# A transformer block with conditioned scales and shifts: the first two modulation vectors made as rows and turned upright

## The reference

```python
mod = silu(c) @ ada_w.T + ada_b                 # c: (2, 576), ada_w: (6*576, 576)
shift_msa, scale_msa, gate_msa, shift_mlp, scale_mlp, gate_mlp = split(mod, 6)
h = rmsnorm(x, g1) * (1 + scale_msa) + shift_msa
q, k, v = split(h @ qkv_w.T + qkv_b)            # q and k are normed per head, times qg and kg
x = x + tanh(gate_msa) * (softmax(q k^T / 6) v @ proj_w.T + proj_b)
h2 = rmsnorm(x, g2) * (1 + scale_mlp) + shift_mlp
x = x + tanh(gate_mlp) * (gelu(h2 @ fc1_w.T + fc1_b) @ fc2_w.T + fc2_b)
```

## Time and profile before

| | |
|---|---|
| median of 3 runs | 2911.23 us (2911.23 to 2912.59) |
| the profiled execution, its own time | 2911.72 us |
| its span, first to last instruction | 2909.9 us |
| busy in the span | PE 99%, PE weight loads 75%, DVE 68%, ACT 54%, POOL 7% |
| mean granted TensorE clock over the span | 0.992 of full speed |
| chain that ended last, by engine | PE 94%, DVE 3%, ACT 1%, DMA 1% |

### The profile page before, as it was taken

The page is one execution under the profiler, slowest core; times in us unless marked ns, Lnnn a source line. Parts: engine busy times, 40 slices in busy tenths (PEclk is TensorE's granted clock), DMA queues, the critical chain, the costliest instruction groups (busy, mean ns, idle before and its releaser), DMA issues.

```text
span 2909.9 us, 35292 instructions
## 1 busy us (share of the span) xinstructions
PE 2878.8 (99%) x12990; PEld 2174.7 (75%) x12990; DVE 1972.3 (68%) x2726; ACT 1578.1 (54%) x1922; POOL 209.9 (7%) x155
## 2 busy tenths in 40 slices
PE   8999999999999999999999999999999999999999
PEld 7999986666666666666666666788888888888887
DVE  7777778899888888888888887844344343434342
ACT  4334326776677677677677666634344343434342
POOL 1323310101000000000000000090000000000000
PEclk8999999999999999999999999999999999999999
DMA  6555554322322222222222223432222222322121
GB/s 229 163 191 172 174 168 132 88 73 63 84 78 77 78 83 63 77 84 78 73 78 69 76 82 91 133 128 86 74 86 74 82 78 90 99 85 86 41 68 50
DMA packets 238454, 282.67 MB, mean 97 GB/s; under 512 B 34960, under 2 KB 144016, under 8 KB 237392
## 3 DMA queue, kind: packets, MB, share of 16 engines
q1 hardware_dynamic: 233696, 271.33, 30.0%
q10 hardware_dynamic: 4592, 9.18, 0.9%
HBM read 195.50 MB, written 84.67 MB: 96 GB/s over the span
## 4 chain that ended last, share of the span: by engine, by line
PE 94%; DVE 3%; ACT 1%; DMA 1%; issue 0%; SPq 0%; DVEq 0%; ACTq 0%
PE ps L1539 16%; PE ps L1564 16%; PE ps L1627 15%; PE ps L1609 15%; PE ps L1551 13%; PE ps L721 12%; PE ps L1585 4%; PE ps L1550 2%; PE ps L685 1%; ACT gated L1230 1%; DMA gain<-kg 0%; DVE p_lo L1356 0%; DVE x L1416 0%; PE ps L677 0%; DVE w_lo L1409 0%
## 5 line engine op out<-in xcount | busy, mean ns | idle before, releaser
L1174 ACT ACTIVATE p_r<-ps 128x1024 f32<-128x1024 f32 x512 | 491.9, 1025 | 406.4 <-PE ps L1539 406.4
L1356 DVE TENSOR_TENSOR p_lo<-p_r,p_hi 128x1024 fp32r<-128x1024 f32 x512 | 613.4, 1219 | 0.0
L1539 PE MATMUL ps<-qT,kT 110*128 110x512 f32 x2048 | 574.9, 398 | 1.4 <-DVE aw L614 0.9
L1174 ACT ACTIVATE prob<-ps 128x1024 f32<-128x1024 f32 x512 | 483.6, 1031 | 2.3 <-PE ps L1539 2.0
L1539 PEld LDWEIGHTS ps<-qT,kT 110*128 110x128 f32 x2048 | 382.9, 190 | 136.3 <-issue 51.4
L1550 PE MATMUL ps<-prob,vp 128*64 128x512 f32 x1024 | 453.1, 595 | 0.0
L1551 PE MATMUL ps<-prob,vp 128*37 128x512 f32 x1024 | 451.7, 594 | 0.0
L1486 DVE TENSOR_TENSOR a_lo<-act,a_hi 128x512 fp32r<-128x512 f32 x144 | 101.2, 702 | 506.0 <-ACT a_hi L1217 506.0
L1350 DVE CAST p_hi<-p_r 128x1024 fp32r<-128x1024 f32 x512 | 350.2, 694 | 134.9 <-ACT p_r L1174 133.5
L1627 PE MATMUL ps<-a_hi,w 128*128 128x512 f32 x1296 | 415.5, 393 | 0.0
L1564 PE MATMUL ps<-p_hi,vx 128*128 128x512 f32 x1024 | 404.6, 395 | 0.1
(11 more groups left out here) (177 smaller groups left out, 3552.7 us busy)
## 6 DMA issues: line engine op xcount, KB each, us to landing
w_raw<-w SPq DMA_DIRECT2D x144, 320.0 KB, 2.8
qk_hi_scratch<-aw SPq DMA_DIRECT2D x32, 576.0 KB, 3.2
qk_lo_scratch<-aw SPq DMA_DIRECT2D x32, 576.0 KB, 4.4
kT<-qk_hi_scratch SPq DMA_DIRECT2D x128, 144.0 KB
qT<-qk_hi_scratch SPq DMA_DIRECT2D x128, 144.0 KB
v_scratch<-stv SPq DMA_DIRECT2D x32, 512.0 KB, 2.6
vp<-v_scratch SPq DMA_DIRECT2D x16, 1024.0 KB, 9.1
xb<-xT SPq DMA_DIRECT2D x8, 1280.0 KB, 10.7
```

Source lines behind the costliest of these rows:

```text
L1174: act.activation(out, ps[:, 2 * slot:2 * slot + 2, :].rearrange("p a b -> p (a b)"), ACT.Exp).then_inc(exp_done, 1)
L1356: dve.tensor_tensor(p_lo[:, j], p_r[:, j], f32(p_hi[:, q % HIGHS]), ALU.subtract).then_inc(plo_done, 1)
L1539: mm = pe.matmul(ps[:, 2 * (entry % RING) + h, :], kT[r][:, h, kt * P:(kt + 1) * P], qT[:, u % 2, h], start=True, stop=True)
```

## The change

Both modulation vectors are now made in one manner on PE: the two columns of silu(c) are the stationary operand and the modulation weights move past it, 512 and 64 columns at a time, so that each of five steps over the inputs gives two rows (one for each sample) of 576 outputs. ACT copies the rows out of PSUM into a place in `xb[:, 1]` (`rows_out`), and five small matmuls with an identity turn them upright, onto the partitions (`upright`). DVE's dot products for the shift are gone from the opening and from the first tile. The four loads of single numbers and the load of the biases are one load (`small`). The tokens are loaded second, ahead of the shift's weights; the load of the second sample's tokens waits until both vectors are upright, since the rows use its place. The squares are added up as ACT delivers them, and `bounded` stands ahead of the first `w_low`. PE spreads silu(c) for sample 1 after the norm is spread, in front of the first tile.

```diff
         sp.dma_start(c_t[:], cT).then_inc(c_ld, 16)
-        sp.dma_start(adab_t[:], adab).then_inc(small_ld, 16)
-        sp.dma_start(awp, ada).then_inc(aw_ld[1], 16)
-        sp.dma_start(aws, adan[0]).then_inc(aw_ld[0], 16)
+        sp.dma_start(small_t[:], small).then_inc(small_ld, 16)
+        sp.dma_start(by_rows[0], ada[0]).then_inc(aw_ld[0], 16)
         sp.dma_start(xb[:, 0], xT[:, :, 0:BLK]).then_inc(x_ld[0], 16)
-        for j in range(4):
-            sp.dma_start(gain[:, j:j + 1], gains[j].partition_broadcast(P)).then_inc(gain_ld, 16)
+        sp.dma_start(by_rows[1], ada[1]).then_inc(aw_ld[1], 16)
         load_w(0)
         load_w(1)
         load_w(2)
         load_w(3)
+        sp.dma_start(bias[:], qkvb.partition_broadcast(P)).then_inc(bias_ld, 16)
         sp.wait_ge(zero_done, 1)
         sp.dma_start(m_s.rearrange("m (a n) -> m a n", a=B * N // BLK),
                      f32(h_lo[0:2 * H, 1, 0]).unsqueeze(1).to_broadcast([2 * H, B * N // BLK, BLK])).then_inc(zero_dma, 16)
+        sp.wait_ge(mod_mm, 2)
         sp.dma_start(xb[:, 1], xT[:, :, N:N + BLK]).then_inc(x_ld[1], 16)
-        sp.wait_ge(dot_done, KC + 2)
-        sp.dma_start(bias[:], qkvb.partition_broadcast(P)).then_inc(bias_ld, 16)
-        sp.wait_ge(mod_mm, 1)
-        sp.dma_start(awn, adan[1]).then_inc(awn_ld, 16)
+        sp.wait_ge(rows_mm, 1)
+        sp.dma_start(awn, adan[0]).then_inc(awn_ld, 16)
         sp.dma_start(pb_t[:], pb).then_inc(late_ld, 16)
         sp.dma_start(f2b_t[:], f2b).then_inc(late_ld, 16)
         sp.dma_start(f1b_t[:], f1b).then_inc(late_ld, 16)
...
+        def spread_c(b):
+
+            act.wait_ge(cb_mm, b + 1)
             act.activation(c_b[:, b, 0:KF * P], ps[:, 6 + b, :], ACT.Copy).then_inc(cb_done, 1)
-        act.activation(c_b[:, :, KF * P:D], CT, ACT.Copy).then_inc(cb_done, 1)
-
+            act.activation(c_b[:, b, KF * P:D], CT[b], ACT.Copy).then_inc(cb_done, 1)
+
+        def rows_out(j):
+
+            act.wait_ge(rows_mm, j + 1)
+            act.activation(mrow[:, j, 0:KF * P], ps[0:B, 2 * j, :], ACT.Copy).then_inc(rows_done, 1)
+            act.activation(mrow[:, j, KF * P:DP].rearrange("p (a c) -> p a c", a=2),
+                           ps[0:B, 2 * j + 1, 0:TL].unsqueeze(1).to_broadcast([B, 2, TL]), ACT.Copy).then_inc(rows_done, 1)
+
+        spread_c(0)
         act.wait_ge(x_ld[0], 16)
         for m in range(KC):
+            if m == KF - 1:
+                rows_out(0)
             act.activation(tmp[:, m], xb[:, 0, m], ACT.Square).then_inc(sq0_done, 1)
         split_w(0)
         norm_act(act, 0)
         split_w(1)
+        rows_out(1)
         for m in range(KC):
             act.wait_ge(aff_done, m + 1)
+            act.wait_ge(modn_add, B)
             act.activation(h_hi[:, 0, m], tmp[:, m], ACT.Identity,
                            bias=mod[:, SHIFT_MSA, m, 0:1], scale=1.0).then_inc(hhi0_done, 1)
+            if m == 0:
+                spread_c(1)
             if m == 1:
                 split_w(2)
         split_w(3)
...
+        def sum_first():
+
+            for k in (1, 2):
+                dve.wait_ge(sq0_done, k + 1)
+                dve.tensor_tensor(tmp[:, 0], tmp[:, 0], tmp[:, k], ALU.add).then_inc(sqsum, 1)
+                dve.wait_ge(sqsum, k)
+            dve.wait_ge(sq0_done, KF)
+            dve.tensor_tensor(tmp[:, 0], tmp[:, 0], tmp[:, KF - 1], ALU.add).then_inc(sqsum, 1)
+            dve.wait_ge(sqsum, KF - 1)
+            dve.wait_ge(sq0_done, KC)
+            dve.tensor_tensor(tmp[0:TL, 0], tmp[0:TL, 0], tmp[0:TL, KF], ALU.add).then_inc(sqsum, 1)
+            dve.wait_ge(sqsum, KF)
+            dve.tensor_copy(sq_hi[:], tmp[:, 0]).then_inc(sqhi_done, 1)
+            dve.wait_ge(sqhi_done, 1)
+            dve.tensor_tensor(sq_lo[:], tmp[:, 0], f32(sq_hi[:]), ALU.subtract).then_inc(sqlo_done, 1)
...
-        dve.wait_ge(cb_done, 3)
-        dve.wait_ge(aw_ld[0], 16)
-        for m in range(KC):
-            shift(0, m, bias[:, 0:D])
-        for m in range(2):
...
-        dve.wait_ge(gain_ld, 64)
+        dve.tensor_scalar(root_gain[:], gain[:, 0:1], float(D) ** 0.5, None, ALU.mult).then_inc(gain_b, 1)
         dve.tensor_scalar(qscale[:], gain[:, 2:3], gain[:, 3:4], float(HD) ** 0.5, ALU.mult,
                           ALU.mult).then_inc(gain_step, 1)
...
-        dve.wait_ge(sq0_done, KC)
-        sum_chunks(dve, 0)
-
-        dve.tensor_scalar(root_gain[:], gain[:, 0:1], float(D) ** 0.5, None, ALU.mult).then_inc(gain_b, 1)
+        sum_first()
         dve.wait_ge(mod_mm, 1)
         dve.wait_ge(adab_one, 1)
-        dve.tensor_tensor(mod[:, SCALE_MSA], MOD1, adab_t[:, KC:2 * KC].unsqueeze(2).to_broadcast([P, KC, B]),
+        dve.tensor_tensor(mod[:, SCALE_MSA], MODT[0], adab_t[:, KC:2 * KC].unsqueeze(2).to_broadcast([P, KC, B]),
                           ALU.add).then_inc(mod_done, 1)
         dve.wait_ge(gain_b, 1)
         dve.wait_ge(mod_done, 1)
         dve.tensor_scalar(mod[:, SCALE_MSA], mod[:, SCALE_MSA], root_gain[:, 0:1], None, ALU.mult).then_inc(mod_done, 1)
+        bounded(dve, 0)
         w_low(0, 0, wlo_done)
-        bounded(dve, 0)
         reciprocal(dve, 0)
         w_low(0, 1, wlo_done)
         dve.wait_ge(mod_done, 2)
-        dve.wait_ge(modn_add, 1)
         dve.wait_ge(rb_mm, 1)
         scaled(0)
+        dve.wait_ge(mod_mm, 2)
+        dve.tensor_tensor(mod[:, SHIFT_MSA], MODT[1], adab_t[:, 0:KC].unsqueeze(2).to_broadcast([P, KC, B]),
+                          ALU.add).then_inc(modn_add, B)
         w_low(1, 0, wlo_done)
+        dve.wait_ge(modn_add, B)
         h0_low(0)
         scaled(1)
         w_low(1, 1, wlo_done)
...
-                    if first and r == 0 and t == 0:
-                        for m in range(2, KC):
-                            shift(1, m, prod)
...
     def pe_part(pe):
-        def modulate(m):
-
+        def modulate(j, ks):
+
+            for k in ks:
+                rows = slice(0, P if k < KF else TL)
+                for bank, cols in ((2 * j, slice(0, KF * P)), (2 * j + 1, slice(KF * P, D))):
+                    mm = pe.matmul(ps[0:B, bank, 0:cols.stop - cols.start], c_s[rows, k], by_rows[j][rows, k, cols],
+                                   start=k == 0, stop=k == KC - 1)
+            return mm
+
+        def upright(j):
+
+            pe.wait_ge(rows_done, 2 * j + 2)
+            for m in range(KC):
+                mm = pe.matmul(MODT[j][:, m], mrow[:, j, m * P:(m + 1) * P], ident[0:B, 0:B], start=True, stop=True)
+            mm.then_inc(mod_mm, 1)
+
+        def spread_c(b):
+
+            wait(pe, cb_done, 2 * b)
             for k in range(KC):
                 rows = slice(0, P if k < KF else TL)
-                mm = pe.matmul(MOD1[:, m], awp[rows, k, m * P:(m + 1) * P], c_s[rows, k],
-                               start=k == 0, stop=k == KC - 1)
-            return mm
+                out = ps[:, 6 + b, k * P:(k + 1) * P] if k < KF else CT[b]
+                mm = pe.matmul(out, c_s[rows, k, b:b + 1].to_broadcast([P if k < KF else TL, P]),
+                               ident[rows, rows], start=True, stop=True)
+            mm.then_inc(cb_mm, 1)
 
         def sum_squares(i):
 
@@ -685,22 +719,20 @@
                 mm = pe.transpose(TP[:, c * P:(c + 1) * P], stq[:, t % 2, c * P:(c + 1) * P], ident[:])
             mm.then_inc(turn_mm, 1)
 
-        pe.wait_ge(c_silu, 1)
+        pe.wait_ge(silu_step, 4)
         pe.wait_ge(ident_done, 1)
-        for b in range(B):
-            for k in range(KC):
-                rows = slice(0, P if k < KF else TL)
-                out = ps[:, 6 + b, k * P:(k + 1) * P] if k < KF else CT[:, b]
-                mm = pe.matmul(out, c_s[rows, k, b:b + 1].to_broadcast([P if k < KF else TL, P]),
-                               ident[rows, rows], start=True, stop=True)
-        mm.then_inc(cb_mm, 1)
+        spread_c(0)
+        pe.wait_ge(aw_ld[0], 16)
+        modulate(0, range(KC)).then_inc(rows_mm, 1)
+        upright(0)
         pe.wait_ge(aw_ld[1], 16)
```

More of the change, by code:

```diff
@@ L109, in build @@
         first = FirstUnit(nc, ctx, qk_hi, qk_lo, v_s, m_s)
-        parts = qkv_phase(nc, ctx, sb, ps, first, xT, cT, ada, adan, adab, wqkv, qkvb, pb, f1b, f2b, gains, qk_hi, qk_lo, v_s, m_s,
-                  ident, ones, mod, gate_b, gain, qscale, bound, unbounded, pb_t, f2b_t, f1b_t)
+        parts = qkv_phase(nc, ctx, sb, ps, first, xT, cT, ada, adan, small, wqkv, qkvb, pb, f1b, f2b, qk_hi, qk_lo, v_s, m_s,
+                  ident, ones, mod, gate_b, small_t, adab_t, gain, qscale, bound, unbounded, pb_t, f2b_t, f1b_t)
         main_phase(nc, ctx, ps, first, parts, qk_hi, qk_lo, v_s, m_s, l_s, oh_s, ol_s, xT, w2, wp, w1, outT, ident, ones, unbounded, bound, mod, gate_b,
@@ L154, in load_v, with qkv_phase @@
         sp.dma_start(self.vp[:], self.v_s[0:NT, :, 0:VP].rearrange("t p c -> p t c")).then_inc(self.v_ld, 16)
-def qkv_phase(nc, ctx, sb, ps, first_unit, xT, cT, ada, adan, adab, wqkv, qkvb, pb, f1b, f2b, gains, qk_hi, qk_lo, v_s, m_s,
```

(13 more changed lines are left out.)

65 lines of the change are left out of this document (29 added, 36 removed).

## The result

| | before | after |
|---|---|---|
| median (6 runs each, same chip) | 2911.89 us (2911.23 to 2912.66) | 2922.72 us (2921.39 to 2922.97) |
| profiled execution, own time; its span | 2911.72; 2909.9 us | 2922.71; 2920.9 us |
| mean granted clock | 0.992 | 0.997 |

The ratio is 1.0037, 95% interval 1.0027 to 1.0047: 10.8 us slower, where 3.9 us faster was forecast. The forecast's range ended at 2915.0.

What follows compares the result with a forecast made beforehand. The kernel was taken as nearly all PE-bound from 34.40 us, behind the load of kg, so the opening counts by the first tile's end: 46.5 to 42.55 us. 2911.72 less 3.9 gives 2907.8 us, range 2904.5 to 2915.

Steps and rivals of the forecast that it cites:

- Behind that the phase repeats itself and moves as it is: After the opening and first tile: later work keeps its timing, apart from clock changes worth 0.3 us better or worse.
- First vector on PE: Opening: five pairs of matmuls start at 7.8 us, full clock from 11.6, done by 14.6, rows copied by 15.4.
- Rival 1: Opening: the clock doesn't rise for matmuls with two weight columns; first tile 8.0 us later, about 2919.5 us; chance 14%.
- Rival 2: Opening: the clock rises, then falls in the break for the rows at 14.6 us; gain 1.1, 2910.6 us; chance 12%.
- Loads: Opening: tokens land at 11.3 us instead of 15.3; without the lull, the first weight piece at 18.5 instead of 21.3.
- Rival 3: Opening: the DMA lull stays, not being the gain loads'; first piece at 20.9 us, total 2910.6 us; chance 7%.
- h0_low: End of the opening: this step ahead of the first tile starts at 26.7 us instead of 30.2.
- The first tile's end: First qkv tile: w_low ends at 39.4 us, then the last 16 matmuls take 3.15, ending at 42.55 instead of 46.5.
- A clock that fell for some microseconds between would be hidden by these waits: First tile: a temporary clock fall costs nothing, because PE waits on DVE there anyway.
- the term of 3.9 us: Whole kernel: the saving taken from 2911.72 us, from the first tile ending at 42.55 instead of 46.5 us.
- Second sample's tokens and POOL: Start of qkv phase: tokens land near 33.5 us, needed at 35.4; POOL ends at 47.4, PE asks at 48.1; both hidden.
- rival 5: Tile 1: second sample's tokens over 2 us late or POOL slowed, giving back 1 to 3 us, 2909.8; chance 7%.

Runs made afterwards that it cites:

- e1: The kernel before plus one unused tile of 128 bytes a partition, shifting the main phase's bottom-placed tiles as in the changed kernel: 2925.38 us, ratio 1.0048.
- e2: The changed kernel with biases and gain back in their old tiles, so every tile stands where it stood before the change: 2908.58 us, ratio 0.9993.
- e3: The kernel before with only fc2's moving operands a_hi and a_lo 128 bytes higher: 2923.06 us, ratio 1.0040.
- m4: TensorE alone, running MLP and attention matmul sequences at several kernels' addresses: an MLP matmul took 0.2287 us (before), 0.2309 (e1), 0.2316 (e3), 0.2286 (e4), 0.2267 (e7).
- e5: e4 with each of the four qkv weight pieces starting at a multiple of 256 bytes: 2907.55 us, ratio 0.9986.
- e6: The kernel before with its four gain loads replaced by one load, places kept: 2911.01 us, ratio 0.9999.
- e8: e7 with all four qkv weight pieces 192 bytes over a multiple of 256: 2903.11 us, ratio 0.9973.
- e7: e2 with all tiles placed from the top of SBUF 192 bytes lower: 2906.58 us, ratio 0.9984.
- e10: e8 with the attention's tiles over w2 back on their old places: 2898.95 us, ratio 0.9959.
- e4: e2 with fc2's moving operands a_hi and a_lo 192 bytes higher: 2909.25 us, ratio 0.9992.
- e9: The kernel before with only the top tiles 192 bytes lower, as in e7: 2909.60 us, ratio 0.9993.

## Why the prediction was wrong

**The step that failed** is the sentence "Behind that the phase repeats itself and moves as it is", and with it the assumption that "from there the timeline moves as a whole". I had costed every instruction and transfer of the diff, and no tile. Against -2.6 us by the end of the qkv phase (-2.3 at the first tile's end) stand +3.4 in the attention and +10.1 in the MLP: 10.9 of the 11.0 us between the spans. That both come from places is shown by e1 and e2, for the MLP by e3 and m4 as well. None of the five rivals was this one; the rival on the slow side, at 14%, was another (the clock), and it did not happen. The chance of 12% for slower thus named the wrong mechanism too.

The other steps, one by one:
- *First vector on PE*: five pairs took 7.87 us from 7.79; at 1.96 us a pair at half clock and 0.98 at full that is three slow and two fast ones, so the clock rose near 13.6, not at 11.6. Rows copied by 16.4 instead of 15.4. Rival 1, no rise for two weight columns, fell: the granted clock read full, and the second vector's three pairs took 3.07 us. That column read full from the start in both kernels, so the rise is seen in the spacing alone. Rival 2, a fall in the break for the rows, did not come in this profile, where PE stood idle for 0.83 us from 15.65. That was luck in part: in e5's profile, with the same opening, the clock read 0.51 from 17.8 to 21.2 us behind the same break of 0.83, and the three pairs took 4.77 us.
- *Loads*: first piece at 18.55, forecast 18.5; tokens at 12.20 for 11.3, hidden. The lull is gone, by e6 the gain loads' doing. Rival 3 fell. Its estimate of 0.34 us from the Trainium skill ("DMA: Bandwidth & Descriptors", section "Bandwidth") is worked out wrongly: the page has its 10.5 ns for the packets of a whole transfer, not for those of one engine, so there is nothing to divide by 16. An estimate from it is then 512 x 10.5 ns = 5.4 us, and against that stands the lull of 2.4 us that the rows gave.
- *h0_low*: 27.35 for 26.7, late by what the clock's rise cost, part of it hidden.
- *The first tile's end*: DVE's `w_low` ended at 40.06 (39.4 plus the same delay), and half 1 was to wait for it. In e2, whose profile shows the full clock throughout this stretch, `w_low` ended at 40.45 and DVE took the half 3.52 us later, at 43.97; by that it would have been 43.58 here, and it was 44.27. The clock fell to 1.2 GHz while PE waited 1.95 us for the second `h0_low`, as windows of after show (us, busy, PEclk, DMA share, GB/s):

```profile
28.00:31.00 3.00, 1.45 (x6) 0.91 1.04 387
31.00:34.00 3.00, 2.45 (x7) 0.50 1.10 438
34.00:37.00 3.00, 3.00 (x10) 0.50 0.76 264
```

  "A clock that fell for some microseconds between would be hidden by these waits" was wrong by 0.7 us here. Whether it holds depends on the profile: of the six others with this opening, e2 and e8 show no fall here, e7 and e10 a shorter one that was hidden, e4 and e5 one that cost as much as in the changed kernel. The Trainium skill ("TensorE: Matmul & The Clock Gate", section "HAM oscillation — how this bites in real kernels") describes a kernel whose bursts of matmuls are shorter than the waits between them, so that each burst starts slow. In the changed kernel's profile the trace agrees in this place, where 1.4 us of work stand ahead of the wait of 1.95; in e2's, with the same work and wait, it does not.
- So the term of 3.9 us (3.95 for the tile) measured 2.3 in this profile: 0.65 went by the late rise, 0.7 by the fall, and 0.3 because the last 16 matmuls and their hand-over to DVE were put too low (3.15 us for the 3.4 of e2). On the old places it is 2.8 by the medians of e2, and e7 less e9 gives 3.0. The mechanism was right, the size off.
- *Second sample's tokens and POOL*: ACT took them at 36.03 without a wait and POOL ended at 48.0, before the 49.75 us at which PE used the sums; rival 5 fell.
